# Windowed attention on one core: scores and value products in four parts a tile, and a new order of steps

## What is computed

```python
for i in range(DEPTH):                       # 6
    x = attn_layer(shift_tokens(x), Wqkv[i], q_scale[i], k_scale[i], Wo[i]) + x
    x = ffn_layer(shift_tokens(x), ln_g[i], ln_b[i], W1[i], b1[i], W2[i], b2[i]) + x
```

## Time and profile before

| | us |
|---|---|
| median of 3 runs | 3975.99 |
| lowest, highest | 3974.95, 3983.92 |
| the profiled execution | 3987.9 |
| its span, first to last instruction | 3986.1 |
| TensorE busy | 3633.8 |
| scalar, vector engine busy | 2766.0, 2734.0 |
| GpSimd busy | 1037.4 |

### The profile page before, as it was taken

How to read it: one execution, slowest core, us unless ns; L and a number is a source line. 1 busy time by engine, 2 the same in 40 slices (tenths; PEclk the granted TensorE clock), 3 DMA queues, 4 the chain that set the end, 5 groups by cost and what they waited for, 6 DMA issues and landing times.

```text
span 3986.1 us, 157311 instructions
## 1 busy us (share of the span) xinstructions
PE 3633.8 (91%) x64569; PEld 2525.9 (63%) x64761; DVE 2734.0 (69%) x5376; ACT 2766.0 (69%) x9073; POOL 1037.4 (26%) x857
## 2 busy tenths in 40 slices
PE   6776999999999999999999999999999999999997
PEld 3333666666666666666666666666666666666665
DVE  3334777777777777777777777777777777777774
ACT  3443776776777776777777677777777777777775
POOL 0001232232232233232223223223223223223220
PEclk7556999999999999999999999999999999999998
DMA  1001555445455445455545454545554545544452
GB/s 49 7 7 31 115 115 121 108 106 137 105 119 122 107 111 136 107 121 117 116 111 125 114 125 105 124 106 123 122 117 109 120 112 123 115 114 110 111 121 68
DMA packets 361465, 421.61 MB, mean 106 GB/s; under 512 B 52480, under 2 KB 266000, under 8 KB 360000
## 3 DMA queue, kind: packets, MB, share of 16 engines
q1 hardware_dynamic: 360768, 411.67, 44.8%
HBM read 19.30 MB, written 2.10 MB: 5 GB/s over the span
## 4 chain that ended last, share of the span: by engine, by line
PE 77%; ACT 9%; issue 5%; DVE 0%; SPq 0%; DMA 0%; POOL 0%; DVEq 0%; ACTq 0%
PE ring_ps L1062 18%; PE out_ps L1176 8%; PE ring_ps L1109 7%; PE score_ps L1127 7%; PE out_ps L1204 7%; PE out_ps L1164 7%; ACT probs L659 6%; PE turn_ps L1146 6%; PE turn_ps L1138 4%; PE small_ps L1073 4%; PE turn_ps L1211 2%; PE score_ps L1117 2%; ACT att_t L647 1%; ACT L641 1%; PE out_ps L1194 1%
## 5 line engine op out<-in xcount | busy, mean ns | idle before, releaser
L659 ACT ACTIVATE probs<-score_ps,neg_max,rq 128x64 f32<-128x64 f32 x3072 | 1191.7, 418 | 185.9 <-DVE neg_max L876 184.7
L838 DVE TENSOR_TENSOR prod<-ring_ps,tables 128x512 f32<-128x512 f32 x1536 | 951.4, 681 | 157.3 <-PE ring_ps L1062 146.5
L532 POOL TENSOR_TENSOR ks<-prod 128x1024 f32<-128x1024 f32 x192 | 451.5, 2352 | 2102.8 <-DVE prod L838 2018.6
L1062 PE MATMUL ring_ps<-xs,wqk 128*128 128x256 f32 x3072 | 765.7, 387 | 11.9 <-DVE xs L825 5.1
L614 ACT ACTIVATE square<-ring_ps,biases 128x512 f32<-128x512 f32 x768 | 507.1, 687 | 252.0 <-DVE prod L838 229.7
L659 ACT ACTIVATION_READ_ACCUMULATOR probs<-score_ps,neg_max,rq 128x1 f32 x3072 | 673.6, 219 | 0.0
L1062 PEld LDWEIGHTS ring_ps<-xs,wqk 128*128 128x128 f32 x3072 | 555.5, 191 | 116.3 <-issue 41.1
L647 ACT ACTIVATE att_t<-turn_ps 128x512 f32<-128x512 f32 x384 | 229.3, 597 | 501.0 <-PE turn_ps L1146 501.0
L532 POOL TENSOR_TENSOR qs<-prod 128x1024 f32<-128x1024 f32 x192 | 451.9, 2354 | 243.5 <-DVE prod L838 235.9
L1164 PE MATMUL out_ps<-v,pt 64*32 64x64 f32 x24576 | 349.7, 224 | 88.5 <-issue 87.1
L1109 PE MATMUL ring_ps<-wv,xs 128*128 128x512 f32 x768 | 405.5, 631 | 1.0 <-issue 1.0
(11 more groups left out here) (156 smaller groups left out, 4483.7 us busy)
## 6 DMA issues: line engine op xcount, KB each, us to landing
v<-vs SPq DMA_DIRECT2D x1344, 128.0 KB
qt<-qs SPq DMA_DIRECT2D x768, 128.0 KB
kt<-ks SPq DMA_DIRECT2D x768, 128.0 KB
v<-vs SPq DMA_DIRECT2D x192, 64.0 KB
wqk<-in_L_ffn_Wqkv SPq DMA_DIRECT2D x6, 1024.0 KB, 5.2
wv<-in_L_ffn_Wqkv SPq DMA_DIRECT2D x6, 512.0 KB
wo<-in_L_ffn_Wo SPq DMA_DIRECT2D x6, 512.0 KB
prod<-in_L_attn_x SPq DMA_DIRECT2D x16, 128.0 KB, 2.1
```

The lines of the kernel that those rows point to most:

```text
L532: pool.tensor_tensor(dst, prod_a[p % 2], prod_b[p % 2], ALU.add).then_inc(rot_ready, 1)
L659: last = nc.scalar.activation(probs[i][:, j, e, :], score_ps[e][:, KEYS * j:KEYS * (j + 1)], ACT.Exp, bias=neg_max[:, h:h + 1], scale=rq[p ...
L838: last = V.tensor_tensor((prod_b if a else prod_a)[p % 2][:, f, :] .rearrange("p (u c) -> p u c", u=2), bank[:, :].rearrange("p (u c) -> p ...
L1062: last = mm(bank_of(s, parity)[:, TOKENS * f:TOKENS * (f + 1)], wqk[:, n, 2 * c + f, a, :], xs[:, WINDOW:PADDED], start=True, stop=True)
```

## The change

Scores and value products are issued in quarters: S00, S01, S02, S03 are each two head pairs of tile 0 (16 matmuls, 64 instructions), S10 to S13 those of tile 1, and PV likewise. The mask is still written ahead of part 0, and the semaphore is counted up behind part 3. PV waits for the first copy of the transposes at part 0 and for the second at part 2. `alone(pe)` is gone at TU, KN, S00 and PV. All five lists but SP's are new: in TensorE's, S00 stands between PA0 and PB0, S12 and S13 between PB3, UP1 and TU, T00 ahead of PA2, TU ahead of UP2, TQ behind V3, KN0 and KN1 together behind PV00, V2 behind PV10.

```diff
--- before.py
+++ after.py
@@ -47,19 +47,19 @@
 
 
 PE_ORDER = """
-PA0 PB0 S00 S01 PA1 PB1 BI WO PA2 PB2 CEN NK T00 VAR PA3 TK PB3 UP0 S10 S11 UP1 UP2 TU T01 NQ KN0 PV00 DN KN1
-PV01 TQ T10 V0 V1 T11 PV10 O00 PV11 V2 O01 V3 O10 O11
+PA0 S00 PB0 S01 S02 S03 PA1 PB1 BI WO T00 PA2 CEN NK PB2 TK VAR S10 S11 PA3 UP0 PB3 S12 UP1 S13 TU UP2 NQ T01
+PV00 KN0 KN1 DN PV01 PV02 PV03 T10 V0 V1 T11 PV10 V2 O00 PV11 PV12 PV13 O01 V3 TQ O10 O11
 """
 DVE_ORDER = """
-XS RA0 RB0 M0 RA1 RB1 BI XA XB RA2 RB2 CK XG TC00 RB3 RA3 H0 M1 H1 H2 UC TC01 CQ KM0 X KM1 TC10 AT0 TC11 VC1 AT1
+XS RA0 RB0 M0 RA1 RB1 BI XA XB RA2 CK RB2 XG TC00 RA3 RB3 H0 M1 H1 H2 UC TC01 KM0 KM1 X AT0 TC10 TC11 CQ VC1 AT1
 VC3
 """
 ACT_ORDER = """
-QA0 QB0 E00 QA1 QB1 E01 E02 SQ QA2 QB2 LN E03 RTK LG G0 QB3 QA3 G1 G2 LE E10 E11 E12 E13 VC0 RTQ OC00 OC01 VC2
+QA0 QB0 E00 E01 QA1 QB1 E02 SQ E03 QA2 LN QB2 RTK LG G0 QA3 QB3 G1 G2 LE E10 E11 E12 E13 VC0 VC2 OC00 OC01 RTQ
 OC10 OC11
 """
 POOL_ORDER = """
-AD0 AD1 AD2 RK AD3 TB
+AD0 AD1 RK AD2 AD3 TB
 """
 SP_ORDER = """
 LK MQ MK LV LL MV
@@ -1083,7 +1083,6 @@
                 if kind == "TU":
                     pe.wait_ge(rk_parts, at(g, 4, 4))
                     bank_free(g, s)
-                    alone(pe)
                     turn = bank_of(s, parity)[0:3 * HEADS, 0:TOKENS // 2].bitcast(BF16)
                     for i in range(TILES):
                         last = pe.transpose(turn[:, P * i:P * (i + 1)],
@@ -1110,17 +1108,16 @@
                        start=True, stop=True).then_inc(v_made, 1)
                 if kind == "S":
 
-                    i, half = s[1], s[2]
-                    if half == 0:
+                    i, part = s[1], s[2]
+                    if part == 0:
                         pe.wait_ge(exp_ready, at(g, TILES * PARTS, PARTS * i))
                         for e in range(2):
                             mm(score_ps[e][:, :], ident_bf[:, :], mask_bf[:, i, :, :].rearrange("p j c -> p (j c)"),
                                start=True, stop=False, skip_group_check=True)
-                    if i == 0 and half == 0:
+                    if i == 0 and part == 0:
                         pe.wait_ge(k_moved, moved(g, 1))
                         pe.wait_ge(q_moved, moved(g, 1))
-                        alone(pe)
-                    for j in range(PAIRS // 2 * half, PAIRS // 2 * (half + 1)):
+                    for j in range(PAIRS // 4 * part, PAIRS // 4 * (part + 1)):
                         for w in range(WPT):
                             for e in range(2):
                                 q0 = P * i + WINDOW * w
@@ -1128,7 +1125,7 @@
                                           qt[64 * e:64 * e + 64, j, q0:q0 + WINDOW],
                                           kt[64 * e:64 * e + 64, j, q0:q0 + KEYS],
                                           start=False, stop=True, skip_group_check=True)
-                    if half == 1:
+                    if part == 3:
                         last.then_inc(s_ready, 1)
                 if kind == "T":
                     i, c = s[1], s[2]
@@ -1147,9 +1144,10 @@
                                             att[i][:, 4 * c + j, :, :].rearrange("p e k -> p (e k)"), ident[:, :])
                     last.then_inc(o_made, 1)
                 if kind == "PV":
-                    i, half = s[1], s[2]
-                    pe.wait_ge(t_copied, at(g, 2 * TILES, 2 * i + half + 1))
-                    if half == 0:
+                    i, part = s[1], s[2]
+                    if part % 2 == 0:
+                        pe.wait_ge(t_copied, at(g, 2 * TILES, 2 * i + part // 2 + 1))
+                    if part == 0:
                         if i == 0:
                             if g == 0:
                                 pe.wait_ge(v2_zeroed, 1)
```

## The result

The changed kernel takes 4047.4 us (4046.1 to 4049.8), the kernel before 3975.5 (3974.0 to 3983.9): ratio 1.0177, interval 1.016 to 1.0195. I had forecast 4001: the sign was right, the size a third of what came.

What follows compares the result with a forecast made beforehand. TensorE bounds the kernel, losing 1.63 us a batch to instruction fetch. 35.41 + 0.5 + 0.22 + 0.27 + 0.1 = 36.5, plus 0.8 of stalls = 37.3 against 37.04 a batch: median 4001 us, range 3925 to 4060.

Steps and rivals of the forecast that it cites:

- Stall-free batch: One batch without instruction-fetch stalls: 35.41 us before, forecast 36.5 us after (36.2 to 36.9).
- (d): Moved steps on the other engines' queues, walked through one batch at timeline durations: price 0, kt's slack 0.8 us.
- (a): Three more runs of small matmuls on TensorE, all before UP2: 0.17 us each (0.1 to 0.25), 0.5 a batch.
- (c): TQ moved into the tail after T11: +0.27 us; its reader RTQ ahead of OC10: +0.1 us (0 to 0.5).
- (b): TU moved ahead of UP2: its 0.22 us counts in full, work taken out after UP2 becomes wait at T11.
- (e): Eight semaphore instructions leave TensorE's queue: 0, at most 0.4 us a batch.
- (f): Instruction-fetch stalls before scores and value products: from 1.63 to 0.8 us a batch (0.15 to 1.6).
- kt: Moves of kt, issued later behind AD3, land 0.5 us into the next batch, needed at 1.3: price 0.
- A: Rival: stalls half gone, order dearer, 4001 us; chance 0.42.
- rival C: Stalls and order cancel, stalls at 0.4 to 0.6 us a batch: 3976 us; chance 0.18.
- B: Rival: fetch truly evened out, 0.15 us of stalls left, order priced as forecast: 3939 or 3919 us; chance 0.30.
- D: Rival: nothing won, block ends still meet runs of 192 or kt lands late: 4080 us; chance 0.10.

Runs made afterwards that it cites:

- e4: The changed kernel with GpSimd's addition AD0 started only when neg_max of tile 0 has ended: 3979.1 us, 0.9992 of the kernel before.
- e6: The kernel before with GpSimd's addition AD0 held until tile 0's scores are done: 4018.0 us, 1.0091 of the kernel before.
- E00: Not a run but a step of the kernel: the first exponentials of tile 0, which follow neg_max of tile 0.
- e2: e1 with the scores spread (S00 ahead of PB0, S12 and S13 between UP1 and UP2): 4020.3 us, 1.0158 of the kernel before.
- e13: e12 with VectorE's H0 one step earlier, ahead of RB3: 1.0052 of the kernel before.
- e12: e4 with each tile's scores in one piece again, behind PB0 and ahead of PA3: 4047.7 us, 1.0160 of the kernel before.
- e9: e4 with GpSimd's order back to AD0 AD1 AD2 RK AD3: 0.9968 of the kernel before.
- e1: The changed kernel's code with the old order of steps, quarters side by side, alone(pe) increments gone: 3952.8 us, 0.9924 of the kernel before.
- e10: e1 run once more, beside a run with two increments put back elsewhere: 0.9939 of the kernel before.
- e5: e4 with GpSimd's addition AD2 also started only behind neg_max of tile 1: 4242.5 us, 1.0718 of the kernel before.
- e3: e1 with the value products spread as in the changed kernel, scores in one piece, no run added: 3919.9 us, 0.9840 of the kernel before.
- e8: e3 with the transpose O11 set behind the next batch's PA0, and VC3 behind the next XS: 3865.0 us, 0.9758 of the kernel before.
- e15: e8 with T00 behind UP2, its copy TC00 behind H2 and T01 behind NQ: 3912.9 us, 0.9835 of the kernel before.
- e16: e13 with GpSimd's old order AD0 AD1 AD2 RK AD3: 1.0035 of the kernel before.

## Why the prediction was right and wrong

**Stall-free batch: 36.5 forecast, 37.2 measured.** The measured time lies inside my range, the change was to be 25 us and was 72. The failed step is **(d)**, the walk through the queues at the timeline's durations, priced 0. It took neg_max at the length it had in its old surroundings and gave it that length in the new. The walk had AD0 and S00 in their new places, and so had everything needed to see that the addition would be in flight when neg_max is due. Freeing this one step (e4) gave back 68 us, nearly all of the result; putting it into the kernel before (e6) cost 39. What the walk should have held in place of 0: neg_max of tile 0 at 1.23 us, ending when AD0 ends, and with it E00 at 6.73 behind PA0 (6.05 in the kernel before, 5.69 in e4), which makes T00 wait 0.42 and the quiet batch 0.79 longer. That e4's quiet batch, 36.43, is the 36.5 of the sum is in part luck: (a) was too low and (c) too high. Without the hold the forecast of 25 us would have missed too, for the kernel then stands level with the one before. The Trainium skill, "SBUF — State Buffer", section "Who interferes with whom", states the rule that I didn't weigh: "A DVE instruction with two SBUF inputs contends with a GpSimd instruction that reads SBUF", and "Issue order, not op shape, decides who blocks". The traces agree: neg_max has two inputs in SBUF, and in all 187 cases of the changed kernel's trace in which it lasted over 0.2 us it ended 30 to 39 ns behind a GpSimd addition that had begun before it; the row maxima, read from PSUM, took 693 ns at most over GpSimd's additions and 691 away from them. The row of L876 before, 174/371/1240, was there to be read.

**(a) Runs.** 0.17 each forecast, 0.20 and 0.23 measured (e2), inside the range of 0.1 to 0.25; the third run has no figure of its own. Missing was that S00 ahead of PB0 pushes PB0, its product and its squares, and PB1 waits 0.27 for its bank: a moved step's followers, again.

**(b) TU.** The mechanism holds: UP2's end to T11 is 8.26 in the quiet batches of every kernel tabled but e13. But of TensorE's 0.47 us more between WO and UP2's end in e4 (15.16 for 14.69), TU's 0.22 among it, not all could be had back: in the quickest batch of e4 H0 ends only 0.26 ahead of UP2's start, and e12 shows the wait for it. The T11 wait of 0.9 in nearly every batch did not come. PV00 waits for H2 first (56.7 us), and T11 is then just in time. The 43.3 us of L1135, the sign I had named, look like it and are not: 38.2 of them are T00's waits behind the first hold, and T11 waits once (2.5 us). e9 shows that PV00's wait and T11's are one slack: with H2 early, T11 waits 0.50 in 85 batches.

**(c) TQ and RTQ in the tail.** 0.37 forecast; T11 to PA0 in quiet batches is 6.98 for 6.87: 0.1. Over-priced. In the quickest batches TQ takes its 0.26 and RTQ ahead of OC10 costs 0.02 (O11 waits 0.71 for 0.69), but T11 to O01, with V2 now between PV10 and O00, takes 3.53 for 3.75. The order of the four value runs gave back 0.22, which I had left out.

**(e) The increments.** 0 forecast. They were worth 0.6 to 0.8% in the old order (e1, e10), all of it outside the quiet batches, where I had not looked for it. Nor were they eight: two stand-alone instructions a batch are gone, because waits that had hung on the increments now stand alone instead.

**(f) Stalls.** 0.8 a batch left forecast, 0.41 measured (mean 37.62, taken as in the prediction, less quickest 37.21). The size was off to the good: 28.1 for 40 on the values and 5.7 for 20 on the scores. I had said the scores keep theirs; e12 against e4 shows that, with the other steps placed as here, the split takes 37 us off them. My factor of 1.45 for "what they drag" hid a mechanism: a good part of it is the lower clock behind the long stalls, which does not shrink in proportion but was gone altogether. And my condition (184 instructions in under 4 us) is needed rather than enough: of the block ends that I can place in the trace before, 169 meet it and 64 of these stalled (by over 0.5 us), as did 5 of the 223 others.

**kt.** Its landing was rightly no cost; e5 shows the edge, and that kt lands 1.8 us behind the end of its issue (1260.26 to 1262.04), where I had taken 1.7.

**Rivals.** A was the nearest, with its terms as said but the hold left out. The kernel without the hold, e4, stands at 3979: that is rival C, the cancelling of stalls and order, which I had given 0.18. B's condition (stalls under 0.5) was met, its price list wasn't. D's late kt came only in e5.

## What to carry to other kernels

An instruction whose duration at one shape spreads as here, from 0.17 to 1.24 us, may be waiting inside: find what runs beside it before moving anything, and price the move by what will be in flight then, not by its old median. Spread small matmuls first where a run exists already and only its length changes (e3, 0.8% over e1); a split that adds a run cost 0.2 us here and pushes what follows the step that it overtakes. When a wait is taken away, follow the freed step to the next reader, and what is delayed to the last transfer behind it: of eight such edits here (e4, e5, e8, e9, e12, e13, e15, e16) three (e4, e8, e9) went by the first theory that I had written down. A stall of TensorE can cost more than its own length: look at the granted clock in the microseconds behind it.

## What the runs showed of the hardware that I had not expected

VectorE's scaling of a 128x16 tile, 0.17 us, lasted up to 2.05 us beside GpSimd's additions of 128x1024 (2.35 us each), and ended 30 to 39 ns behind them; products, maxima and copies with at most one input in SBUF were not lengthened (prod: 693 ns at most, alone and over GpSimd). Behind stalls of 1.8 to 2.6 us TensorE's granted clock fell to 1.2 GHz in 16 places of the kernel before, at about 1.6 us each; the changed kernel, whose longest stall in the layers is 1.7 us, has none. One or two semaphore instructions a batch in TensorE's stream moved the whole by up to 0.8% with the length of the quiet batches unchanged.
